# Self-attention scores: from eight masked heads over the whole array to four heads in each row half, with the keys spread by ScalarE

## The reference, cut to what matters

```
q_h, k_h, v_h = (x @ Wq)[:, h], (x @ Wk)[:, h], (x @ Wv)[:, h]    # 56 x 16 each
p_h = softmax(q_h @ k_h.T * 0.25)                                 # 56 x 56
y   = concat_h(p_h @ v_h) @ Wo;  x = x + y
```

## Time and profile before

| | |
|---|---|
| median of 3 runs | 2299.67 us (2297.08 to 2299.9) |
| the profiled execution | 2300.18 us, its span 2298.5 us |
| mean granted TensorE clock | 0.855 of full |
| PE / DVE / ACT / POOL busy | 72% / 72% / 46% / 32% |
| bit, its tiles | about 48 to 350 us of the span |
| rot, its tiles | about 1530 to 1812 us |
| causal, its tiles | about 1834 to 2040 us |

### The profile page before, as it was taken

The page is one execution under the profiler, slowest core; times in us unless marked ns, Lnnn a source line. Parts: engine busy times, 40 slices in busy tenths (PEclk is TensorE's granted clock), DMA queues, the critical chain, the costliest instruction groups (busy, mean ns, idle before and its releaser), DMA issues. The chain is left out here.

```text
span 2298.5 us, 35379 instructions
## 1 busy us (share of the span) xinstructions
PE 1650.9 (72%) x11032; PEld 956.4 (42%) x11032; DVE 1646.5 (72%) x2628; ACT 1051.3 (46%) x1629; POOL 740.1 (32%) x586
## 2 busy tenths in 40 slices
PE   1444448779999999999977458636767477756893
PEld 0222226433333333333327447524445345534682
DVE  6988882558988988988976843368778456547474
ACT  0433341456566666566643434335555243435362
POOL 1211110023343343343400445424334234336242
PEclk9766665689999999999998579869898799986897
DMA  7700000011111111111100244410000100013234
GB/s 222 255 0 0 0 0 14 7 30 45 38 36 44 33 40 44 29 44 43 31 9 15 75 141 137 139 51 1 0 0 0 25 1 0 0 56 102 67 114 138
DMA packets 78309, 116.34 MB, mean 51 GB/s; under 512 B 11617, under 2 KB 59161, under 8 KB 77811
## 3 DMA queue, kind: packets, MB, share of 16 engines
q1 hardware_dynamic: 70451, 94.00, 14.5%
q0 software_dynamic: 7776, 21.28, 2.6%
HBM read 60.38 MB, written 40.19 MB: 44 GB/s over the span
## 5 line engine op out<-in xcount | busy, mean ns | idle before, releaser
L1699 ACT ACTIVATE lat_Pb<-banks 125x896 f32<-125x896 f32 x384 | 344.9, 917 | 275.5 <-PE banks L1625 267.4
L1762 DVE TENSOR_TENSOR lat_dsum<-lat_dsum,lat_Pb 125x896 f32<-125x896 f32 x320 | 410.9, 1284 | 26.2 <-ACT lat_Pb L1699 20.1
L1585 PE MATMUL banks<-lat_Pb,lat_kv 125*64 125x448 f32 x1536 | 331.7, 553 | 0.0
L1618 PE MATMUL banks<-lat_QH,lat_kT 128*125 128x448 f16 x768 | 204.8, 370 | 48.2 <-ACT lat_Pb L1699 42.7
L1541 POOL TENSOR_TENSOR lat_kk<-lat_rot,lat_kk 125x768 f16<-125x768 f32 x32 | 52.5, 1640 | 400.9 <-ACT lat_kk L1675 400.9
L1618 PEld LDWEIGHTS banks<-lat_QH,lat_kT 128*125 128x125 f16 x768 | 80.5, 137 | 191.1 <-ACT lat_Pb L1699 157.5
L1585 PEld LDWEIGHTS banks<-lat_Pb,lat_kv 125*64 125x64 f32 x1536 | 93.5, 136 | 153.9 <-issue 153.5
L2066 POOL DMA_INDIRECT sent_outputs<-moe_yb,moe_yidx x98 | 99.1, 1011 | 153.2 <-ACT moe_yb L2307 125.6
L2202 PE MATMUL banks<-moe_w2d,moe_gT 88*128 (+3 forms) x780 | 107.7, 290 | 18.1 <-DVE moe_gT L2486 12.3
L1625 PE MATMUL banks<-lat_QL,lat_kT 64*125 64x448 f16 x768 | 114.6, 377 | 0.0
L1759 DVE TENSOR_TENSOR lat_dsum<-lat_Pb 125x896 f32<-125x896 f32 x32 | 60.7, 1898 | 74.5 <-ACT lat_Pb L1699 74.5
(11 more groups left out here) (410 smaller groups left out, 3797.3 us busy)
## 6 DMA issues: line engine op xcount, KB each, us to landing
moe_xb<-sent_rows SPq DMA_DIRECT2D x49, 257.0 KB
lat_raw<-in_ctx_dram SPq DMA_DIRECT2D x32, 375.0 KB
moe_arena<-sent_outputs SPq DMA_DIRECT2D x16, 512.0 KB, 7.5
sent_rows<-zero SPq DMA_DIRECT2D x1, 7453.0 KB, 47.4
lat_QH<-lat_QT SPq DMA_DIRECT2D x64, 112.0 KB, 2.2
lat_QL<-lat_QT SPq DMA_DIRECT2D x64, 112.0 KB, 2.2
sent_rows<-zero SPq DMA_DIRECT2D x1, 5140.0 KB, 63.5
sent_outputs<-zero SPq DMA_DIRECT2D x1, 4096.0 KB, 38.2
```

What stands on the lines that cost most here:

```text
L1585: ins = nc.tensor.matmul(ps[u * DC:(u + 1) * DC, 4 + par, 0:8 * T], kv[:, par, tt, :], Pb[:, tt % NPB, u, :], start=tt == 0, stop=tt == KT ...
L1618: nc.tensor.matmul(ps[0:KP, 2 * (tt % 2) + u, 0:8 * T], kT[:, par, tt, 0:KP], queries(QH, u), start=True, stop=False)
L1699: nc.scalar.activation(Pb[:, tt % NPB, :, :], ps[0:KP, 2 * (tt % 2):2 * (tt % 2) + 2, 0:8 * T], ACT.Exp, scale=1.0 / QSCALE).then_inc(exp_ ...
L1762: ins = nc.vector.tensor_tensor(dsum[:, par], dsum[:, par], Pb[:, tt % NPB], ALU.add)
```

## The change

The projection's columns are put in another order, so that after the transposition block c of q and of k holds, on partitions 0 to 63, heads 4c to 4c+3 and, on partitions 64 to 127, heads 8+4c to 8+4c+3. The order is made by a reading pattern of the weights (`in_halves`); in bit the quantised weights are written in that order, and in rot the bias row is copied once in that order (`bqk`). ACT no longer copies k: it reads `QKT` four times with a scale for each partition (`m4`: one for the partitions of the head m of each four, zero else; in rot `hgm`, gain and bias times it) and writes `Km` of half the size. The maskings on DVE and POOL are gone, with their waits. The scores are eight fp32 matmuls of 64 rows, 64 columns and 224 moving columns, in each c one for each row half a and sequence b, into bank 4+a. In causal the four mask matmuls are issued together ahead of them. An increment by PE's sequencer (`s_begun`), for which nothing waits, is put behind the waits.

```diff
-        qT, kT = sb("qT", [P, 2, P]), sb("kT", [P, 2, P])
-        Km = sb("Km", [P, 2, 2, 8, T])
+        qT = sb("qT", [P, 2, P])
+        Km = sb("Km", [P, 2, 2, 4, T])
+        m4 = sb("m4", [P, 4])
+        hgm = sb("hgm", [P, 4, 2]) if rot else None
...
+        def in_halves(w):
+            return w.rearrange("p (a q e) -> p q a e", a=2, q=2)
...
-                        masked_keys(nc.gpsimd, 1).then_inc(km2_made, 1)
-                        pool.wait_ge(km2_made, i + 2)
...
                         if live(i):
                             act.wait_ge(s_done, i + 1)
-                            act.wait_ge(km_made, i + 1)
-                            act.wait_ge(km2_made, i + 1)
-                        for c, dst in ((2, kT), (0, qT)):
-                            if rot:
-                                ins = nc.scalar.activation(dst[:], QKT[:, c:c + 2, :], ACT.Identity,
-                                                           scale=hgb[:, 0:1], bias=hgb[:, 1:2])
-                            else:
-                                ins = nc.scalar.activation(dst[:], QKT[:, c:c + 2, :], ACT.Copy)
-                            ins.then_inc(qT_made, 1)
+                        kT = QKT[:, 2:4, :].rearrange("p c (b t) -> p c b t", b=2)[:, :, :, 0:T]
+                        for m in range(4):
+                            scale = hgm[:, m, 0:1] if rot else m4[:, m:m + 1]
+                            bias = hgm[:, m, 1:2] if rot else 0.0
+                            nc.scalar.activation(Km[:, :, :, m, :], kT, ACT.Identity, scale=scale,
+                                                 bias=bias).then_inc(km_made, 1)
+                        if rot:
+                            ins = nc.scalar.activation(qT[:], QKT[:, 0:2, :], ACT.Identity,
+                                                       scale=hgb[:, 0:1], bias=hgb[:, 1:2])
+                        else:
+                            ins = nc.scalar.activation(qT[:], QKT[:, 0:2, :], ACT.Copy)
+                        ins.then_inc(qT_made, 1)
...
+                        pe.sem_inc(s_begun, 1)
...
+                        for c in range(2):
+                            for a in range(2):
+                                rows = slice(a * HALF, (a + 1) * HALF)
+                                for b in range(2):
+                                    ins = nc.tensor.matmul(
+                                        ps[b * HALF:(b + 1) * HALF, 4 + a,
+                                           c * 4 * T:(c + 1) * 4 * T],
+                                        qT[rows, c, b * HALF:(b + 1) * HALF],
+                                        Km[rows, c, b, :, :].rearrange("p h t -> p (h t)"),
+                                        start=not causal, stop=not causal or c == 1)
...
+                then(nc.vector.tensor_tensor(m4[:], hmask[:, 0:4], hmask[:, 4:8], ALU.add))
+                if rot:
+                    for u in range(2):
+                        then(nc.vector.tensor_copy(
+                            bqk[:, u].rearrange("p (q a e) -> p q a e", a=2, q=2),
+                            in_halves(brow[:, u * D:(u + 1) * D])))
+                    then(nc.vector.tensor_tensor(
+                        hgm[:], m4[:].unsqueeze(2).broadcast_to([P, 4, 2]),
+                        hgb[:].unsqueeze(1).broadcast_to([P, 4, 2]), ALU.mult))
+                dve.sem_inc(m4_made, 1)
...
-                        then(nc.vector.tensor_scalar(dst, wm, -1.0, None, ALU.max))
+                        if m < 2:
+                            for c in range(2):
+                                then(nc.vector.tensor_scalar(
+                                    dst[:, c].rearrange("p (q a e) -> p q a e", a=2, q=2),
+                                    in_halves(wm[:, c]), -1.0, None, ALU.max))
+                        else:
+                            then(nc.vector.tensor_scalar(dst, wm, -1.0, None, ALU.max))
...
-                def mask_keys(i):
-
-                    dve.wait_ge(qT_made, 2 * (i + 1))
-                    masked_keys(nc.vector, 0).then_inc(km_made, 1)
```

More of the change, by code:

```diff
@@ L294, in self_attention @@
         yo = sb("yo", [P, D])
-        own, own_pool, km2_made = sem("dve"), sem("pool"), sem("second_keys_masked")
+        own, own_pool, m4_made = sem("dve"), sem("pool"), sem("masks_made")
+        s_begun = sem("scores_begun")
         loaded, prepared, dve_prepared = sem("weights_loaded"), sem("pads_zeroed"), sem("weights_made")
@@ L673, in scores @@
                     if live(i + 1):
-                        pe.wait_ge(km_made, i + 2)
-                        pe.wait_ge(km2_made, i + 2)
-                        pe.wait_ge(qT_made, 2 * (i + 2))
+                        pe.wait_ge(km_made, 4 * (i + 2))
+                        pe.wait_ge(qT_made, i + 2)
                         if live(i):
                             pe.wait_ge(centered, i + 1)
-                        for c in range(2):
-                            if causal:
+                        pe.sem_inc(s_begun, 1)
+                        if causal:
+                            for a in range(2):
                                 for b in range(2):
-                                    nc.tensor.matmul(ps[b * HALF:(b + 1) * HALF, 4 + c, 0:8 * T],
+                                    nc.tensor.matmul(ps[b * HALF:(b + 1) * HALF, 4 + a, 0:8 * T],
                                                      idb[:, b * HALF:(b + 1) * HALF],
@@ L686, in scores @@
                                                      start=True, stop=False)
-                            for b in range(2):
-                                ins = nc.tensor.matmul(
-                                    ps[b * HALF:(b + 1) * HALF, 4 + c, 0:8 * T],
-                                    qT[:, c, b * HALF:(b + 1) * HALF],
-                                    Km[:, c, b, :, :].rearrange("p h t -> p (h t)"),
-                                    start=not causal, stop=True)
+                        for c in range(2):
+                            for a in range(2):
+                                rows = slice(a * HALF, (a + 1) * HALF)
[6 more added lines that the diff above has]
+                                        start=not causal, stop=not causal or c == 1)
                         ins.then_inc(s_done, 1)
@@ L761, in body @@
                                 for c in range(2):
-                                    ins = nc.tensor.matmul(PJ[:, lo:hi], xT[:, 1, c, :], wq[:, c, lo:hi],
+                                    w = wq[:, c, lo:hi]
+                                    ins = nc.tensor.matmul(PJ[:, lo:hi], xT[:, 1, c, :],
+                                                           in_halves(w) if lo == 256 else w,
                                                            start=c == 0, stop=c == 1)
@@ L765, in body @@
                             for lo in (0, 256):
+                                w = wkv[:, lo:lo + 256]
                                 ins = nc.tensor.matmul(PJ[:, 256 + lo:512 + lo], cT[:],
[L767 removed]
+                                                       w if lo else in_halves(w), start=True,
+                                                       stop=True)
                         ins.then_inc(proj_done, 1)
@@ L1027, in body @@
                         center(i)
-                    if live(i + 1) and causal:
-                        mask_keys(i + 1)
                     if live(i + 1) and rot:
@@ L1046, in body @@
                         add_output(i - 1)
-                    if live(i + 1) and not causal:
-                        mask_keys(i + 1)
                     if live(i - 1) and bit:
```

33 lines of the change are left out of this document (7 added, 26 removed).

## The result

The changed kernel takes 2312.58 us in the median of 4 runs (2311.02 to 2316.67), the kernel before 2298.38 beside it (2295.95 to 2299.9): a ratio of 1.0066, 95% interval 1.0048 to 1.0083. It is slower, by 14 us, and the forecast of 2310 stood 2.6 us under it.

What follows compares the result with a forecast made beforehand. No engine filled the span; each stage had a limit of its own. Bit +5.3, causal +9.3, rot -6 and once-costs +1.7 gave +10.3 us on 2300.2, so 2310 us, range 2295 to 2327.

Steps and rivals of the forecast that it cites:

- The spread, 0.345 and 0.43: ScalarE's four scaled copies of k: 0.345 us each in bit and causal, 0.43 in rot.
- Bit, +0.35 a tile: Bit stage: ScalarE's 1.10 us more, less 0.76 idle before yT's copy, leaves 0.35 us a tile on the path.
- the sum: Whole kernel: 15 periods of each stage's change plus once-costs, +10.3 us on 2300.2, giving 2310.
- once-costs: Setup done once a stage, such as bit's weight writings, m4 and rot's small steps: together 1.7 us (0.5 to 3).
- Causal, +0.62 a tile: Causal stage: ScalarE's 1.10 us more, less 0.48 of slack before yT's copy, leaves 0.62 us a tile.
- rival B: TensorE's clock falls in causal, with rot 0.7 us slower a tile: 2340, or 2325 with one; chance 0.14.
- Rot, -0.4 a tile: Rot stage: shorter scores against later weight copies, gaining 0.85 at full clock or losing 0.7 at low; mean gain 0.4 us.
- rival D: Rot's clock stays up, so rot gains 0.85 us a tile: 2303; chance 0.13.
- Scores, 0.92: TensorE's scores: 16 passes of 224 columns, four at a time, take 0.92 us where all eight took 1.72.
- rival C: Row halves don't overlap, scores stay at 1.7 us and rot loses 0.4 a tile: 2322; chance 0.09.
- Rival A: ScalarE's copies are cheap, a spread costing 0.26 us, so the kernel is faster: 2288; chance 0.12.
- VectorE 50 us less busy for nothing: Sign in the profile after: without its masking, 1.09 us a tile, VectorE is some 50 us less busy, for nothing.

Runs made afterwards that it cites:

- e1: Changed kernel, but ScalarE copies the keys once, VectorE masks all of them and GpSimd masks nothing; ratio to the kernel before 0.9872.
- e2: Changed kernel with every spread made twice, first into a buffer nobody reads; ratio to the kernel before 1.0471.
- e11: Changed kernel with nine dummy matmuls a tile in rot, filling both of TensorE's idle gaps; ratio to the kernel before 0.9990.
- e5: Changed kernel with every row-half matmul of the scores issued twice; ratio to the kernel before 1.0130.
- e7: Order of e4, but in bit and rot ScalarE copies the keys once and VectorE masks them; ratio to the kernel before 0.9730.
- e4: Changed kernel reordered: bit's spreads after yT's copy, causal's exponential before the spreads, rot's scores between PE's rounds; ratio to the kernel before 0.9684.
- e6: Changed kernel in which GpSimd still makes its old masking product, into a buffer nobody reads; ratio to the kernel before 1.0072.

## Why the prediction was right, and what in it was not

- **The spread, 0.345 and 0.43.** Four last 1.44 to 1.46 us of which the last one is 0.446: (1.46 - 0.45) / 3 = 0.337 from start to start, and 0.43 in rot. The Trainium skill's 0.37 (ScalarE: Activation LUTs, What ACT_TABLE_LOAD costs) is 0.03 too long for these.
- **Bit, +0.35 a tile.** Right in size and in mechanism: 0.40 in the steady mean, by ScalarE's chain at yT (e1, e2). Over 15 periods it was +3.6 for the 5.3 of the sum, since the first and last tiles gain.
- **What the sum left out: the start of bit.** The first maximum came 4.6 us earlier; I worked in steady tiles only. Before, VectorE waited there 3.17 us for the copies of q and k, made its half of the masks (1.09), and its next instruction, L985 of the norm, took 1.78 beside GpSimd's first mask, where the same took 0.41 after. The changed kernel has none of this, and its once-costs, which I did count, bring 0.95 (the first copy of keys starts that much later): 3.17 + 1.09 + 1.37 - 0.95 = 4.68. That is how much earlier the instruction behind it starts, 46.69 (last line) for 51.37, and from there to the first maximum VectorE works without a wait in both kernels. The first scores, of 3.25 us, ended at 54.54, 3.2 before that maximum, and had no part in it:

```profile
48.55 1.09 DVE L392 TENSOR_TENSOR bit_Km<-bit_kT,hmask 128x896 f32<-128x896 f32 x1 [3.17 <-ACT bit_qT L543]
49.56 1.78 DVE L985 TENSOR_SCALAR bit_xtmp<-x_res,bit_stats_mean,bit_stats_r 128x256 f32<-128x256 f32 x1
51.29 3.25 PE L688 MATMUL banks<-bit_Km,bit_qT 128*64 128x448 f32 x8 [3.47 <-POOL bit_Km L392]
```

```profile
46.69 0.42 DVE L989 TENSOR_REDUCE bit_ax<-bit_xtmp 128x1 f32<-128x256 f32 x1
```

- **Causal, +0.62 a tile.** 0.67 in the steady tiles. The rest of its +11.8 (9.3 in the sum) are the first tiles, two of them with a low clock that I had given to rival B only.
- **Rot, -0.4 a tile.** This is the step that failed. At like clock it was right: 17.22 to 16.80 with one low stretch, 16.84 to 16.24 in the second period, with none; and rival D's 0.85 is what 16.37 (e11) is under the 17.22 of the later tile at full clock. But I held the share of low clock for what it had been. The chip granted 1.2 GHz for longer, and rot came out at +0.25; by e11 the clock cost 1.2 us a tile there. The sum did name 0.7 us more in which PE stands idle ahead of the third round, but did not let the clock answer to it. That this gap is the reason is likely by e1 and e11, where it is short or filled and the clock is high, but no run changed it alone. Rival B's mechanism, a falling clock, did happen, in rot (where it named 0.7 a tile and 0.25 came), and in causal only at two places of the first tiles. It was given 0.14 as if it had to come whole.
- **Scores, 0.92.** 0.99, four at a time; rival C is out. That they gain nothing in bit and causal is in the sum, and e5 shows it.
- **Rival A** needed a spread of 0.26. **VectorE 50 us less busy for nothing:** it is 93, since stalls inside instructions beside GpSimd went as well (in bit L1011's alone is 19 us); they were for nothing here because ScalarE took their place in the chain.
- **The total** is nearer than its parts, and that is luck. The sum had +10.3 us and the span grew by 10.8, but over 15 periods bit, rot and causal missed by -1.7, +9.7 and +2.5 us. The early start of bit (4.6), which was not in the sum, and what passed in the stretches between the stages, which no run explains, made up for it.

## What to carry to other kernels

Before work is moved from one engine to another, ask what waits behind it in the queue that it moves to, and whether that queue has a wait long enough a few instructions later: in bit the same four activations in place of one copy cost 1.16 us a tile ahead of a copy that TensorE waited for (e1 against the changed kernel), and 0.07 behind it (e7 against e4). A stall that is removed is worth only the distance to the next chain that ends at the same place, so list both chains before giving it a price. And where TensorE's granted clock already swings from tile to tile, as it did in rot before the change, give the low clock its own term in the forecast, or test it with matmuls that nobody needs.

## What the runs showed that I had not expected

Nine useless fp32 matmuls a tile made rot 1.2 us a tile faster (e11), since the granted clock went from 0.78 to 1.00; where they filled only one of two gaps, it rose to 0.91 or 1.00 by turns. A shorter kernel can have a lower clock: in e1 causal fell to 1.2 GHz in every second or third tile (14.93 us for 12.79), though its undisturbed period was that of before; why there and not in the kernel before is open. The stall of a VectorE product beside GpSimd's went by GpSimd's instruction and not by its own size: 16 columns took 1.53 us before (0.18 alone), and 256 took 1.87 in e6 (0.42 alone), and they ended 0.03 and 0.27 us after GpSimd's did.
